# One-hots with nodes on partitions, made by comparing repeated rows, and attention messages weighed by VectorE

## The reference

```python
# layer 1: attention over edges, 8 heads of 16
k_e = k[src] + attr @ We                   # (edges, 8, 16)
v_e = v[src] + attr @ We
alpha = sum(q[dst] * k_e, per head) / 4
a = exp(alpha - max over the edges of a node)
out[node] = sum over its edges of a * v_e / sum of a

# layer 3: gates
z = logits_src[src] + logits_dst[dst]      # 3 gates of each edge
g = softmax(z)
out[node] = sums over its edges of the gated rows table[src]
```

## Time and profile before

| | |
|---|---|
| median of 3 runs | 5861.45 us (5858.7 to 5862.68) |
| profiled execution | 5857.49 us, its span 5855.7 us |
| mean granted TensorE clock | 0.789 of full speed |
| busy share of the span | PE 68%, DVE 51%, ACT 24%, POOL 59% |
| DMA | 892.81 MB, mean 152 GB/s |

### The profile page before, as it was taken

The page is one execution under the profiler, slowest core; times in us unless marked ns, Lnnn a source line. Parts: engine busy times, 40 slices in busy tenths (PEclk is TensorE's granted clock), DMA queues, the critical chain, the costliest instruction groups (busy, mean ns, idle before and its releaser), DMA issues.

```text
span 5855.7 us, 96074 instructions
## 1 busy us (share of the span) xinstructions
PE 3975.2 (68%) x24005; PEld 3106.2 (53%) x24006; DVE 2994.0 (51%) x9243; ACT 1419.4 (24%) x3648; POOL 3433.6 (59%) x4758
## 2 busy tenths in 40 slices
PE   1000586779996666666675619997998777777774
PEld 0000353446666566566565616665666766666664
DVE  7887510131135667667667652114113566666667
ACT  0012100010013144354443350002002333333333
POOL 7778988830005888888887320000000588888887
PEclk6555798989997798898898769999999655555555
DMA  9961343345545576576676206553552333333332
GB/s 370 368 223 43 120 146 101 124 141 192 192 132 165 168 216 192 180 216 192 183 214 185 71 15 193 189 174 106 191 192 89 97 92 92 92 92 92 92 92 76
DMA packets 537348, 892.81 MB, mean 152 GB/s; under 512 B 92522, under 2 KB 392140, under 8 KB 530910
## 3 DMA queue, kind: packets, MB, share of 16 engines
q1 hardware_dynamic: 420894, 611.37, 32.6%
q0 software_dynamic: 106912, 224.30, 14.1%
q10 hardware_dynamic: 9376, 55.32, 2.7%
HBM read 732.14 MB, written 158.57 MB: 152 GB/s over the span
## 4 chain that ended last, share of the span: by engine, by line
POOL 48%; PE 28%; issue 10%; DVE 7%; DMA 4%; ACT 1%; DVEq 1%; SPq 0%; ACTq 0%; POOLq 0%
PE ps L829 21%; POOL work L381 14%; POOL work L1228 11%; POOL d_adj L501 11%; POOL address L384 5%; POOL hw L1213 4%; PE ps L977 3%; POOL small L505 3%; DMA hw<-d_keys 1%; PE ps L836 1%; DMA d_adj<-logits,address 1%; DVE work L625 1%; PE ps L963 1%; POOL address L1235 1%; ACT work L941 1%
## 5 line engine op out<-in xcount | busy, mean ns | idle before, releaser
L381 POOL DMA_INDIRECT work<-tab_gate,src_col x832 | 797.9, 959 | 1275.9 <-DMA tab_gate<-logits 1141.4
L1228 POOL DMA_INDIRECT work<-tab_kv,src_col x832 | 838.4, 1008 | 748.8 <-DMA tab_kv<-hw 589.4
L829 PE MATMUL ps<-hw 128*128 128x384 bf16 x5096 | 876.1, 333 | 109.7 <-DMA hw<-d_adj 70.6
L829 PE MATMUL ps<-hw,work 128*128 128x384 bf16 x5096 | 866.7, 331 | 78.0 <-DMA work<-d_adj 78.0
L501 POOL DMA_INDIRECT d_adj<-logits,address x782 | 801.9, 1025 | 172.3 <-issue 163.8
L869 DVE TENSOR_TENSOR work<-work,ps 128x128 f32 (+1 forms) x208 | 59.8, 287 | 1487.6 <-ACT work L861 1473.6
L829 PEld LDWEIGHTS ps<-hw 128*128 128x128 bf16 x5096 | 504.9, 100 | 453.9 <-DMA hw<-d_adj 76.7
L829 PEld LDWEIGHTS ps<-hw,work 128*128 128x128 bf16 x5096 | 504.7, 99 | 413.1 <-issue 96.7
L861 ACT ACTIVATE work<-ps 128x128 f32 x208 | 57.6, 277 | 1847.2 <-PE ps L829 1847.2
L1743 PE MATMUL ps<-logits,work 128*128 x1664 | 343.9, 330 | 212.3 <-ACT work L1711 208.2
L1743 PEld LDWEIGHTS ps<-logits,work 128*128 128x128 f32 x1664 | 326.6, 292 | 294.4 <-issue 294.4
(11 more groups left out here) (403 smaller groups left out, 7026.7 us busy)
## 6 DMA issues: line engine op xcount, KB each, us to landing
hw<-d_adj SPq DMA_DIRECT2D x104, 800.0 KB
work<-d_adj SPq DMA_DIRECT2D x104, 800.0 KB
d_adj<-acc SPq DMA_DIRECT2D x52, 1568.0 KB, 21.3
hw<-d_adj SPq DMA_DIRECT2D x104, 768.0 KB
work<-d_adj SPq DMA_DIRECT2D x104, 768.0 KB
work<-attr_dram SPq DMA_DIRECT2D x832, 64.0 KB
d_value<-work SPq DMA_DIRECT2D x208, 256.0 KB
hw<-d_value SPq DMA_DIRECT2D x208, 256.0 KB
```

What stands on the lines that cost most here:

```text
L381: pool.indirect_dma_start(rows[:, r * U + u, 0:width], None, table, bass.IndirectOffsetOnAxis(sources[:, at:at + 1], 0)).then_inc(rows_in[ ...
L829: last = nc.tensor.matmul(at, adj_half[2 * s + hf][:, k, :], xs[:, b, :], start=b == 0, stop=b == BLOCKS - 1)
L1228: pool.indirect_dma_start(rows[:, r * U + u, 0:KV], None, tab_kv, bass.IndirectOffsetOnAxis(src_col[:, at:at + 1], 0)).then_inc(rows_in[r] ...
```

## The change

The one-hot with nodes on partitions is no longer a transpose. The table of relative destinations is written once to DRAM (`d_rel`, a row of 128 edges for each step). In both gather stages SP then loads, for each part, the four rows (512 numbers) repeated to all 128 partitions, straight into the one-hot's buffer (`att_node_hot`, `gate_node_hot`), and DVE compares them in place with its own partition's number (`step_no[:, 0:1]`, a scalar for each partition). Gone are the transposes of one-hots, their copies by ACT, and in the attention stage also the comparison with `iota`. In the gate stage that comparison stays, since the sums need it, and the new one stands ahead of it on DVE. The weighing of the attention messages moves from POOL to DVE for the 168 parts that are weighed within the gathers, four steps to an instruction; POOL now has the memset behind every gather. The tail's 40 parts stay on POOL. The attention loads of `d_rel` stand on SP behind the part's attribute loads; the gate stage's loads have a loop of their own on SP, which had nothing to do there.

```diff
+        d_rel = scratch("d_rel", (STEP_PAD, P))
+        att_node_hot = [part(hot_flat, r * U * P, (U * P,)) for r in range(PARTS)]
+        gate_node_hot = [part((attr_t_flat, hot_t_flat)[r // 2], r % 2 * U * P, (U * P,)) for r in range(PARTS)]
...  # att_load (SP)
+            wait(sp, sem("eq_done"), n - PARTS + 1)
+            sp.sem_inc(sem("turn"), 1)
+            rel_load(sp, att_node_hot[r], n, r)
+        def rel_load(sp, into, n, r):
+            sp.dma_start(into, d_rel[ds(n * U, U), :].rearrange("q e -> (q e)").partition_broadcast(P)).then_inc(rel_in[r], 16)
...
+        def weighed(engine, of, turn, r):
+            engine.wait_ge(sem("exp_ready"), FIRST_PIECE[of + 1])
+            engine.wait_ge(value_in[r], 16 * (turn + FIRST_PART[of] // PARTS + 1))
+            engine.sem_inc(sem("turn"), 1)
+            at = msg_att[:, r * U:(r + 1) * U, 0:D].rearrange("p u (h d) -> p u h d", h=HEADS)
+            return at, part_weights(of, turn, r).unsqueeze(3).broadcast_to((P, U, HEADS, HEAD_DIM))
+        def weigh_dve(dve, of, turn, r):
+            at, wide = weighed(dve, of, turn, r)
+            nc.vector.tensor_tensor(at, at, wide, ALU.mult).then_inc(sem("msg_weighed"), 1)
...  # att_pool
-                    if 0 <= m < TAIL_PART:
-                        weigh_part(pool, m, (u, u + 1))
-                    elif m < 0:
-                        pool.wait_ge(sem("paced"), SPREAD + paced)
-                        paced += 1
-                        pool.memset(pause, 0).then_inc(sem("paced"), 1)
+                    pool.wait_ge(sem("paced"), SPREAD + at)
+                    pool.memset(pause, 0).then_inc(sem("paced"), 1)
...  # att_act, copy
-                nc.scalar.activation(hot_t[:, r % RING2], banks(1), ACT.Copy).then_inc(sem("att_copied"), 1)
...  # att_pe, turn
-                for u in range(U):
-                    last = nc.tensor.transpose(banks(1)[:, u * P:(u + 1) * P], hot[:, r * U + u, :], ident[:])
...  # att_dve
-            def make_hot(n, r):
-                nc.vector.tensor_tensor(hot[:, r * U:(r + 1) * U, :], iota[:].unsqueeze(1).broadcast_to((P, U, P)),
-                                        rel_col[:, ds(n * U, U)].unsqueeze(2).broadcast_to((P, U, P)),
-                                        ALU.is_equal).then_inc(sem("hot_ready"), 1)
+            def make_hot(n, whole, r):
+                dve.wait_ge(rel_in[r], 16 * (whole + 1))
+                nc.vector.tensor_scalar(att_node_hot[r], att_node_hot[r], step_no[:, 0:1], None, ALU.is_equal).then_inc(sem("hot_ready"), 1)
...  # att_dve, step, behind score_part
+                m, of, turn, rm = part_of(k, i, r, WEIGH_BACK)
+                if summed_in_loop(k, m):
+                    weigh_dve(dve, of, turn, rm)
...  # gate_sp, new: waits for gate_logits of the part four back, then
+                rel_load(sp, gate_node_hot[r], n, r)
...  # gate_act and gate_pe lose copy and turn
-            edge_loop(pe, [(1, logits), (3, sums), (0, turn)])
+            edge_loop(pe, [(0, logits), (3, sums)])
...  # gate_dve
-            edge_loop(dve, [(2, logits), (3, message), (2, gates), (0, step_hot(hot_free)), (4, gate_sums.step_add(dve))])
+            def node_hot(i, r):
+                dve.wait_ge(rel_in[r], 16 * (GATE_TURN0 + i + 1))
+                nc.vector.tensor_scalar(gate_node_hot[r], gate_node_hot[r], step_no[:, 0:1], None, ALU.is_equal).then_inc(sem("node_hot_ready"), 1)
+            edge_loop(dve, [(2, logits), (3, message), (2, gates), (0, node_hot), (0, step_hot(hot_free)), (4, gate_sums.step_add(dve))])
...  # setup on SP, ahead of the dense layers
+            sp.dma_start(d_rel.rearrange("(c p) e -> p c e", p=P), edge_f[REL]).then_inc(sem("reset_out"), 16)
```

More of the change, by code:

```diff
@@ L344, in program @@
         attr_in = [sem(f"attr_in{r}") for r in range(PARTS)]
+        rel_in = [sem(f"rel_in{r}") for r in range(PARTS)]
         value_out = [sem(f"value_out{r}") for r in range(2)]
@@ L1199, in tail_sp @@
             edge_loop(sp, [(0, load)], SUM_LAG // PARTS)
[L1201 to L1215, removed]
@@ L1327, in turn @@
                 pe.wait_ge(attr_in[r], 16 * U * (whole + 1))
-                pe.wait_ge(sem("hot_ready"), ATT_HOT0 + n + 1)
-                wait(pe, sem("att_copied"), 2 * n)
+                wait(pe, sem("att_copied"), n)
                 for u in range(U):
-                    nc.tensor.transpose(banks(0)[:, u * D:(u + 1) * D], attr[:, r * U + u, :], ident[:])
-                for u in range(U):
-                    last = nc.tensor.transpose(banks(1)[:, u * P:(u + 1) * P], hot[:, r * U + u, :], ident[:])
+                    last = nc.tensor.transpose(banks(0)[:, u * D:(u + 1) * D], attr[:, r * U + u, :], ident[:])
                 last.then_inc(sem("att_turned"), 1)
@@ L1700, in gate_pool, with gate_sp, load @@
             gathers(pool, GATE_PASS, tab_gate, GATE_ROW, src_col, lambda n: pool.wait_ge(sem("gate_msg"), n + 1))
+        def gate_sp(sp):
+            sp.wait_ge(sem("gate_zeroed"), 2 * GROUPS + 2)
+            def load(i, r):
+                n = i * PARTS + r
+                wait(sp, sem("gate_logits"), n - PARTS + 1)
+                sp.sem_inc(sem("turn"), 1)
+                rel_load(sp, gate_node_hot[r], n, r)
+            for r in range(PARTS):
+                load(0, r)
+            with sp.Fori(1, TURNS) as i:
+                for r in range(PARTS):
+                    load(i, r)
         def gate_act(act):
@@ L1705, in exp @@
                 nc.scalar.activation(gate_exp[r % RING2], gate_z[r % RING2], ACT.Exp).then_inc(sem("gate_exp"), 1)
-            def copy(i, r):
-                n = i * PARTS + r
-                act.wait_ge(sem("gate_turned"), n + 1)
-                wait(act, sem("gate_logits"), n - RING2 + 1)
-                nc.scalar.activation(hot_t[:, r % RING2], banks(0), ACT.Copy).then_inc(sem("gate_copied"), 1)
             def scale(i, r):
@@ L1726, in gate_pe @@
         def gate_pe(pe):
-            def turn(i, r):
-                n = i * PARTS + r
-                pe.wait_ge(sem("hot_ready"), GATE_HOT0 + n + 1)
-                wait(pe, sem("gate_copied"), n)
-                for u in range(U):
-                    last = nc.tensor.transpose(banks(0)[:, u * P:(u + 1) * P], hot[:, r * U + u, :], ident[:])
-                last.then_inc(sem("gate_turned"), 1)
             def logits(i, r):
@@ L1941, in _ @@
             sp.wait_ge(sem("stored"), 16 * (GROUPS + 1))
[L1942 removed]
+            sp.wait_ge(sem("reset_out"), 32)
         @block.gpsimd
```

44 lines of the change are left out of this document (23 added, 21 removed).

## The result

The changed kernel takes 6030.1 us (median of 4 runs, 6027.4 to 6033.4), the kernel before 5862.1 in the same comparison: ratio 1.0287, 95% interval 1.0269 to 1.0304. It is 168 us slower, where 5843 us and a range of 5780 to 5920 were forecast. The profiled execution took 6027.4 us over a span of 6025.5.

What follows compares the result with a forecast made beforehand. The prediction took POOL to set the pace of both gather stages. From 5857.5 us profiled, 74 less in attention and 56 more in the gate stage gave 5839.5, or 5843 us as a median; range 5780 to 5920.

Steps and rivals of the forecast that it cites:

- New waits there: Attention stage: the one-hot waits for its repeated rows, which can be 1.3 us late unseen; counted as nothing.
- The third rival: Attention: repeated rows late or DVE hindered by POOL's locks, a part stays at 6.4 us; 5917 us, chance 0.15.
- attention's other terms: Attention: 114 us less by POOL's pace, 24 more for held gathers, 16 more at the maxima; 74 less.
- The price on the gathers: Attention: DVE's weighing holds the next gather, 0.14 us a part, 24 us; bounds 0 to 116 us.
- the 16 us for the maxima: Attention: each stretch's maximum costs 2.7 us more than before, six times, 16 us.
- The upper bound of 0.69 us a part: Attention: most that held gathers could cost, if the weighing always starts with the gather; 116 us.
- I am wrong if: Signs against the forecast: gate gathers stay at 0.959, L1798 takes 0.69, or DVE no longer waits for rows in attention.
- The gate's term: Gate stage: new comparison delays the iota comparison, which holds a gather; 0.27 us a part, 56 us more, POOL's work unchanged.
- The sign that was named for the gathers: Gate stage: one gather in four of 1.1 to 1.3 us, always the one that meets L394.
- PE's and ACT's saved work: Both gather stages: tile operations and copies taken from PE and ACT lie beside POOL's work; counted at nothing.

Runs made afterwards that it cites:

- weigh_only2: Kernel before with only the weighing of attention messages moved to DVE, memset behind every gather; ratio 0.9849 to the kernel before, at 5863 us.
- loads_ahead: Changed kernel with SP issuing the repeated rows one part ahead and the attributes two parts ahead; ratio 0.9942 to the kernel before.
- weigh_ahead: Kernel before with only the weighing moved to DVE and SP issuing the attributes two parts ahead; ratio 0.9855 to the kernel before.
- gate_tt: Kernel before with the change's gate stage alone, its new comparison written as a two-tensor operation on DVE; ratio 1.0003 to the kernel before, at 6094 us.

## Why the prediction was wrong

The step that failed is "New waits there": it gave the repeated rows 1.3 us of room and counted nothing. Three things in it were wrong. It said that the load is issued "at most one DVE step ahead" and never asked for the least: the load leaves behind the value load, which waits for PE's sums and so for DVE's additions two parts back, and in the timeline it leaves only 0.9 us before DVE is ready for it. The landing was taken as at most 3.0 us from one transfer of 448 KB; the median here is 3.7 us over both stages, 4.2 in attention from 2000 to 3100 us, and 4.3 in the part shown. And lateness was weighed against the slack in one part, where it goes round a loop: kernels with the load in its place take 1495 to 1514 us in attention, with the load one part ahead 1336, which shows the cause. What the term was worth: 1495.2 against 1305.0 in weigh_only2, 190 us, where nothing was counted.

The third rival, DVE's pace by late rows, was what happened, and its price was too small: it let a part stay at 6.4 us and gave 5917. It too had only a limit, DVE's work, and no loop; 13.6 us for two parts gives 6.8, and measured are 6.8 to 7.1 between the maxima and more at each maximum.

The sum of attention's other terms came out: 74 us less was forecast, 74.1 is measured with the weighing alone. That it fits so closely is luck, since two terms were off and made up for each other. The price on the gathers is 0.2 us a part and not 0.14, since a part between the maxima takes 5.96 us on the mean and not 5.90; that is some 10 us more over 168 parts. And 32 parts with one maximum cost about 11 us more than 32 without, before as in weigh_only2, so little is left of the 16 us for the maxima. The upper bound of 0.69 us a part was too high as well: by the earlier trace rows a weighing that starts with a gather holds it for 0.69 + 0.85 - 0.95 = 0.59. The Trainium skill ("SBUF — State Buffer", Who interferes with whom) would have had these gathers undisturbed: they are not, 1.028 against 0.95 us.

In the changed kernel DVE waits for gathered rows for 8.5 us in the attention stage, 230.6 in the earlier trace rows: of the signs named behind "I am wrong if" this one came true.

The gate's term had the right size, but two thirds of it came another way: 56 us forecast, 47 measured. The comparison takes 0.662 us in the median instead of 0.42; it takes that long in the 195 parts where it meets POOL's clearing, and 0.512 in the 11 where it lies within a gather. POOL's loss is mostly not in the gathers (0.018 x 832 = 15 us) but in the clearing (0.039 x 832 = 32 us), which the prediction called untouched. The sign that was named for the gathers, one in four of 1.1 to 1.3 us, is not there: those that meet the iota comparison take 1.01 us. The Trainium skill ("SBUF — State Buffer", Who interferes with whom) has two-port operations, tensor_scalar among them, lock GpSimd out. The trace agrees that they hinder each other, with 0.49 for 0.33 us; but the comparison grew as well (0.66 for 0.48), though it began before the clearing.

That PE's and ACT's saved work is worth nothing stands: loads_ahead, with all of it and the added loads, is as fast in attention as weigh_ahead, with none (1299.0 and 1300.8 us).

The version that beats both kernels is the weighing alone, 5778.5 us, where the kernel before takes 5863; where it takes 6265, that version loses. With every load ahead the node one-hots add nothing to it in attention, and they cost 47 us in the gate stage.

## What to carry to other kernels

Before a new load is put at the end of an in-order queue, follow that queue's own waits back: if one of them leads to the engine that will wait for the load, it is a loop, and its length divided by the parts that it spans is the new pace, whatever slack each engine shows. Here the load cost 190 us in its place and 31 one part earlier, and nothing that could be measured once the attribute loads had moved ahead too. And test parts of a change apart: here a gain of 1.5% was hidden whole behind a loss that came from another edit.

## What the runs showed of the hardware

- A comparison of 128x512 f32 against a scalar per partition takes 0.476 us at least (L1418, median 0.487), seven tenths of the two-tensor form's 0.684 (gate_tt). In the gate stage, where it meets the end of a gather and a clearing, its median is 0.662 us, so little of the advantage is left.
- It stretches a GpSimd clearing that meets it (0.33 to 0.49 us, at most 0.569); a two-tensor operation stretches none (0.329) and holds gathers instead.
- 256 KB of rows repeated to 128 partitions: 3.7 us from issue to landing in the median of the changed kernel, 4.2 in attention and 3.3 in the gate stage. They put 251 GB/s in place of 209 (loads_ahead and weigh_ahead, 2000 to 3100 us), and attention is no longer for it (1299.0 and 1300.8 us).
- One and the same kernel took 5862, 5863, 6265 and 6094 us in different groups of runs, each group within 0.6%, and the weighing's ratio was 0.985 in one and 1.030 in another. The record doesn't show whether the chip decides this: its number is the same for the group of 6265 us and one of those of 5863. A verdict of this size holds for the group in which it is measured.
